# The opening of a two-layer kernel on one NeuronCore: another order for the heads' projections, and layer 1's modulation rows moved to the last leg of attention

## The reference

```
mod = (silu(c) @ wmod).reshape(2, 6, 1, 128)      # sa, ca, ga, sb, cb, gb; ga and gb clamped away from 0
h   = layernorm(x) * (1 + ca) + sa
q, k, v = h @ Wq.T, h @ Wk.T, h @ Wv.T            # 16 heads of width 8
x   = x + ga * softmax(q k^T / sqrt(8)) v
h   = layernorm(x) * (1 + cb) + sb
x   = x + gb * coupling(h)                        # three cycles of a small gelu network and a twist of h
```

## Time and profile before

| | us |
|---|---|
| median of three runs | 1130.92 |
| profiled execution, its own time | 1132.08 |
| its span | 1130.5 |
| mean granted TensorE clock, share of full speed | 0.952 |

### The profile page before, as it was taken

How to read it: one execution, slowest core, us unless ns; L and a number is a source line. 1 busy time by engine, 2 the same in 40 slices (tenths; PEclk the granted TensorE clock), 3 DMA queues, 4 the chain that set the end, 5 groups by cost and what they waited for, 6 DMA issues and landing times. The chain is left out here.

```text
span 1130.5 us, 21410 instructions
## 1 busy us (share of the span) xinstructions
PE 1032.9 (91%) x7835; PEld 647.7 (57%) x7835; DVE 969.4 (86%) x1327; ACT 817.1 (72%) x1593; POOL 518.1 (46%) x487
## 2 busy tenths in 40 slices
PE   6899999999999787989999998899999996499997
PEld 4212222222222233458988885468988984398887
DVE  6889999999995686979999996989999999876766
ACT  3279998999999544978888853988988833246642
POOL 5400441010101121027899982038999984146663
PEclk9769999999999998799999999899999997799999
DMA  5210100001004420108999990108999977612223
GB/s 158 71 40 20 28 18 17 30 16 31 16 2 76 132 57 2 59 1 194 241 246 229 221 213 1 60 22 191 232 246 238 231 185 258 130 54 65 63 63 126
DMA packets 60311, 121.03 MB, mean 107 GB/s; under 512 B 15470, under 2 KB 28782, under 8 KB 59952
## 3 DMA queue, kind: packets, MB, share of 16 engines
q0 software_dynamic: 15440, 52.66, 23.3%
q1 hardware_dynamic: 43034, 64.81, 18.5%
q10 hardware_dynamic: 1734, 2.20, 0.6%
HBM read 58.02 MB, written 13.19 MB: 63 GB/s over the span
## 5 line engine op out<-in xcount | busy, mean ns | idle before, releaser
L2268 PEld LDWEIGHTS m_pair<-filter_w,delta_x_t 128*128 128x128 f32 x2560 | 294.0, 192 | 42.1 <-issue 42.1
L2268 PE MATMUL m_pair<-filter_w,delta_x_t 128*128 128x112 f32 (+3 forms) x2560 | 298.5, 276 | 8.8 <-DVE h_t L2295 3.3
L570 DVE TENSOR_REDUCE neg_max<-max_ps 128x1 f32<-128x1024 f32 x256 | 293.1, 1212 | 10.2 <-PE max_ps L559 10.0
L687 ACT ACTIVATE exp_scores<-score_k 128x512 f32<-128x512 f32 x512 | 273.8, 600 | 19.6 <-PE score_k L679 12.4
L2244 ACT ACTIVATE decay<-delta,a_log 128x1024 f32<-128x1024 f32 x128 | 145.7, 1141 | 49.0 <-DVE normed L2295 28.9
L559 PE MATMUL max_ps<-k_rows,q_rows 48*128 48x512 bf16 x512 | 165.8, 402 | 8.3 <-DVE neg_max L570 7.6
L2236 ACT ACTIVATE filter_w<-filter,b_t 128x112 f32<-128x112 f32 (+1 forms) x576 | 167.4, 374 | 0.0
L707 PE MATMUL score_k<-exp_scores,v_cols 128*32 128x256 f32 x2048 | 164.5, 395 | 0.0
L679 PE MATMUL score_k<-q_rows,k_rows 51*128 51x512 bf16 x512 | 163.5, 390 | 0.0
L579 POOL CAST neg_max_parts<-neg_max 128x16 bf16<-128x16 f32 x16 | 3.1, 197 | 227.8 <-DVE neg_max L570 227.8
L559 PEld LDWEIGHTS max_ps<-k_rows,q_rows 48*128 48x128 bf16 x512 | 29.8, 95 | 120.6 <-DVE neg_max L570 92.6
(11 more groups left out here) (343 smaller groups left out, 1716.3 us busy)
## 6 DMA issues: line engine op xcount, KB each, us to landing
c_row<-c_rows SPq DMA_DIRECT2D x64, 512.0 KB, 6.0
x_inner<-normed POOLq DMA_DIRECT2D x16, 512.0 KB, 6.5
delta_x<-mod_memory POOLq DMA_DIRECT2D x15, 512.0 KB, 8.5
delta_x<-x_inner POOLq DMA_DIRECT2D x15, 512.0 KB, 8.3
x_inner<-h_t POOLq DMA_DIRECT2D x14, 512.0 KB, 6.4
mod_memory<-h_t POOLq DMA_DIRECT2D x14, 512.0 KB, 9.0
mod_memory<-normed POOLq DMA_DIRECT2D x12, 512.0 KB, 8.9
gate_up_all<-in_gate_up_w SPq DMA_DIRECT2D x8, 512.0 KB, 7.4
```

The costliest lines, as they stand in the source:

```text
L570: ve.tensor_reduce(nm[leg % 2][:, 4 * j + qt:4 * j + qt + 1], mps[:, bank:bank + 2, :].rearrange("p a q -> p (a q)"), AX_X, ALU.max, negat ...
L687: ac.activation(pt[a % 4][:, HEADS[r % 4], :], eps[:, bank, :], ACT.Exp, scale=SC).then_inc(*exped.up())
L2268: mm = pe.matmul(vps[blk][:, lo:hi], self.duT[b][:, c, blk * P:(blk + 1) * P], wf[g % 3][:, lo:hi], start=True, stop=True)
```

## The change

It changes the order and the place of work, not what is computed.

1. x of the first batch is loaded in two halves, then the identity and the coupling weights, then the second batch. Statistics, roots and the first eight normalised tiles follow in halves, ahead of the modulation's columns. Layer 1's modulation inputs are loaded after the identity's copy on ACT.
2. The first batch's q and k are split in another division: one middle part on DVE, three on ACT; three low parts on POOL, the last on DVE. Chunk 1 is turned by ACT. Parts of heads 0 to 3 are written out and read back first (all reads issued by SP), those of heads 4 to 15 behind them.
3. All turning, projecting and values of the second batch stand ahead of the first maximum; the 22 tiles ahead are then one stretch. The second batch's middle and low parts and its write to DRAM stand behind.
4. Layer 1's modulation rows, columns, `po_finish_rows(1)` and clamped gate columns leave the front and legs 4 and 5 and go into the last leg, places 0 to 3; the rows are copied out of PSUM by DVE.

`sp_gate_rows` stays where it is.

```diff
+        for half in range(2):
+            lo = half * TB // 2
+            sp.dma_start(self.X[:, lo:lo + TB // 2, :], A["L0_attn_x"][0][lo * P:(lo + TB // 2) * P].rearrange(
+                "(k p) d -> p k d", p=P)).then_inc(*self.in_x[half].up(16))
+        sp.dma_start(self.ident[:], A["k_ident"]).then_inc(*self.in_k.up(16))
...
-            self.ac_load_modulation(1)
...
-            self.ac_silu_c(1)
...
+            self.ac_load_modulation(1)
+            half = TB // 2
+            roots = [self.ln_root(self.X, i * half, (i + 1) * half, [self.in_x[i].at()]) for i in range(2)]
+            self.po_spread(0)
+            normed = [self.ve_ln_apply(self.X, t, roots[t // half]) for t in range(TB)]
+            self.ve_mod_cols(0, cols_ps)
+            scaled = self.m_scale
+            root = self.ln_root(self.X, TB, NT, [self.in_x[2].at()])
...
+                def first_batch_parts():
+                    tiles, rest_in = [(c, side) for c in range(2) for side in range(2)], []
+                    for n, tile in enumerate(tiles):
+                        bank = ring.take()
+                        pe_project(*tile, bank)
+                        ac_part_hi(*tile, bank)
+                        rest_in.append(ve_part_rest(*tile, bank))
+                        if n == 0:
+                            po_part_lo(*tile, ve_part_mid(*tile, rest_in[0]))
+                        if n > 1:
+                            po_part_lo(*tiles[n - 1], ac_part_mid(*tiles[n - 1], rest_in[n - 1]))
+                    ve.wait_ge(*self.ln_aggr.at())
+                    ve_second_batch_normed(range(TB, TB + TB // 2))
+                    ve_part_lo(*tiles[3], ac_part_mid(*tiles[3], rest_in[3]))
+                    ve_second_batch_normed(range(TB + TB // 2, NT))
...
-                for c in range(2):
-                    project(c)
+                first_batch_parts()
                 for c in range(2):
                     values(c)
-                sp_parts_out(0)
-                rows_in[0] = [self.mod_row(0, j) for j in range(4)]
+                sp_parts_out(0, range(4), ((part_hi.at(),), (part_mid.at(), part_ve.at()), (part_po.at(), part_ve.at())))
...
                 for part in range(3):
                     load_first(sp, kp, 1, part)
-                    load_first(ac if part < 2 else sp, qp[:].rearrange("d s a q -> d s (a q)"), 0, part)
+                    load_first(sp, first_q, 0, part)
                 sp_load(0, 1)
-                po.wait_ge(*part_lo.at())
-                po_value_columns()
-                ve.wait_ge(*self.ln_aggr.at())
-                normed += [self.ve_ln_apply(self.X, t, root) for t in range(TB, NT)]
-                self.turn(normed, col(1), col(0), (scaled,), done=ht, by=(0, 0, 0, 1), chunks=(2, 3))
-                rows_in[1] = [self.mod_row(1, j) for j in range(4)]
-                self.ve_mod_cols(1, self.pe_mod_cols(1))
-                ahead(0)
-                project(2)
-                ahead(1)
-                ahead(2)
-                project(3)
+                sp_parts_out(0, range(4, H), ((), (), ()))
+                for j in range(4):
+                    bank = ring.take()
+                    self.pe_mod_row(0, j, bank)
+                    rows_in[0].append(self.ac_mod_row(0, j, bank))
+                turned(2)
+                second_batch_parts(2, 0)
+                turned(3)
+                second_batch_parts(2, 1)
+                for side in range(2):
+                    second_batch_parts(3, side)
                 for c in range(2, NC):
                     values(c)
-                sp_parts_out(1)
-                po.wait_ge(*part_lo.at())
+                self.ac_silu_c(1)
+                for tile, rest_in in rest_known:
+                    po_part_lo(*tile, ac_part_mid(*tile, rest_in))
+                self.po_spread(1)
+                po_value_columns()
                 po_ones(2, NS)
+                for v in range(AHEAD):
+                    ahead(v)
...
+                sp_parts_out(1, range(H), ((part_hi.at(),), (part_mid.at(),), (part_po.at(),)))
...
-                if place == 3:
-                    if leg in (2, 4):
-                        self.po_finish_rows(leg // 2 - 1, rows_in[leg // 2 - 1])
...
-                    if leg in (3, 5):
-                        self.ve_mod_gates(leg // 2 - 1)
+                if place == 3 and leg == 2:
+                    self.po_finish_rows(0, rows_in[0])
+                    m_row0 = self.gate_rows.at()
+                if place == 3 and leg == 3:
+                    self.ve_mod_gates(0)
+                    m_col0 = self.m_col
+                if leg == NLEG - 1:
+                    if place == 0:
+                        ring.bind([mps[:, k, :] for k in range(4)])
+                        pe.wait_ge(*max_read.at())
+                    if place < 2:
+                        for j in (2 * place, 2 * place + 1):
+                            bank = ring.take()
+                            self.pe_mod_row(1, j, bank)
+                            rows_in[1].append(self.ve_mod_row(1, j, bank))
+                    elif place == 2:
+                        self.ve_mod_cols(1, self.pe_mod_cols(1))
+                        self.po_finish_rows(1, rows_in[1])
+                    else:
+                        self.ve_mod_gates(1)
 
             self.ht, self.attn_normed = [], normed
             self.sp_gate_rows()
-            self.ve_coupling_columns()
-            ring.bind([mps[:, k, :] for k in range(4)])
-            pe.wait_ge(*max_read.at())
+            self.ve_coupling_columns(m_row0)
             turn_in(0)
             results(NLEG - 1)
```

More of the change, by code:

```diff
@@ L763, in ahead @@
                 if v == NU + 1:
-                    for m in ring.out():
-                        pe.wait_ge(*m)
+                    pe.wait_ge(*ring.out()[0])
+                    pe.wait_ge(*self.identb_set.at())
                     max_turn(0)
+                    for part in range(3):
+                        sp.wait_ge(*to_dram[0][part].at())
+                    sp.wait_ge(*rows_set.at())
                     for half in range(2):
@@ L882, in attention @@
+                self.po_spread(1)
+                po_value_columns()
+                po_ones(2, NS)
+                for v in range(AHEAD):
+                    ahead(v)
+                for m in ring.out():
+                    pe.wait_ge(*m)
+                sp_parts_out(1, range(H), ((part_hi.at(),), (part_mid.at(),), (part_po.at(),)))
             gated = self.sig("attn_gated")
-            pe.wait_ge(*self.identb_set.at())
-            for v in range(3, AHEAD):
-                ahead(v)
```

122 lines of the change are left out of this document (61 added, 61 removed).

## The result

The changed kernel takes **1139.9 us** (median of 6, 1137.07 to 1142.38) beside 1130.57 for the kernel before (6 runs, 1126.36 to 1133.19): ratio 1.0083, 95% interval 1.0066 to 1.0100, so 9.3 us slower. Its profiled execution took 1138.03 us, span 1136.7, at a mean granted clock of 0.948. The forecast of 1136.5 had the sign right. The measured time lies only 0.1 us inside the upper end of its range (1129.5 to 1140.0) and 0.4 us above the forecast's own range. Against the medians the loss was forecast as 5.6 us and measured as 9.3.

The account below looks back on a forecast made before the run. The prediction took the attention loop's fixed pace, then a chain into coupling, as the bound. From the median 1130.92, - 4.4 (earlier loop) + 9.4 (late swaps) + 0.6 (low clock) gave 1136.5 us, range 1129.5 to 1140.0.

Parts of the forecast that it names:

- The front: Before the attention loop: exponentials begin 4.4 us earlier, 0.7 from the first reduction and 3.7 from sixteen maxima in one stretch.
- x in halves: At the kernel's start: the first chunk is turned by about 11.3 us instead of 12.46, 1.1 us earlier.
- draw: On PE ahead of the first reduction: removing layer 1's rows (4.45 us) balances adding four projections of 0.63 x 2.
- The last leg: At the attention loop's end: layer 1's rows and columns cost PE 2 us, free by themselves because something else is later.
- POOL: In the last leg: POOL finishes layer 1's rows (11.05 us) ahead of the last divide, so DVE gates 2.9 us late.
- SP's queue: At attention's end: the gate rows' write ahead of the swaps makes coupling start 9.4 us later, bounds 4.4 and 10.5.
- Behind it: At coupling's start: PE's next products may run at the low clock, adding 0.6 us, bounds 0 and 2.
- The swaps slip past: Rival, before coupling: the write's traffic doesn't hold the swaps, coupling is only 4.4 us late, 1131.5 us; chance 0.15.
- Absorbed: Rival, in coupling: shorter waits for later swaps take back up to 7.4 of the 9.4 us, 1128.5 us; chance 0.13.
- The front brings nothing: Rival, before the loop: late reads or a clock fall shrink the gain there to 1 us, 1139.9 us; chance 0.10.

## Why the prediction was right, and where it was short

**The front** was right in all its steps. First reduction 30.81 (31.2 predicted), one stretch at 1.18 us, first exponential 56.62 (56.7). Both of its terms are there: 1.1 us at the first reduction (0.7) and 3.4 from the sixteen in one stretch (3.7). With the spread of such landmarks the closeness to a tenth is luck; the 3.6 us over all seven executions lie within the bounds of 2 and 6. The x in halves was put at 1.1 us; the first turned chunk starts at 10.29 for the 11.68 of the earlier trace rows, 1.4 us. The "draw" between the rows and four projections held; the experiment with the rows in front shows what it rests on. With rows, columns and projections all ahead of the first product, the first reduction comes 4.0 us later.

**The last leg** was mis-sized: 2 us for the three blocks on PE, 1.08 + 1.67 + 1.51 = 4.3 measured. The step named a cover ("score banks are filled ahead of ACT") and did not price it. And it was put down as free by itself but for 0.6 us at the root. The term left out DVE: the copies of the rows stand in its queue ahead of the reciprocal that the root hangs on (3.3 us late, shown above).

**A term was missing, in the change's favour:** the gates of layer 1 leave leg 5, where they cost 1.7 us. The page's exponentials alone don't show it; the spacing of one leg's value products against the next would have. From the first exponential to the last value product the loop took 311.2 us against 308.0: + 4.3 for the blocks, - 1.7 for the gates, about - 1.1 for the low stretch of the clock (it reached 10.3 us into the loop instead of 12.8, and ACT is only some half as busy in it), and + 1.7 spread over legs 3 to 5 (20.9, 19.7 and 19.2 us, where 20.5, 18.8 and 18.8 would be the old pattern with one stall). The clock goes with most of that (columns as above):

```profile
138.60:142.00 3.40, 3.40 (x26) 0.56 (x24) 2.81 (x3) 2.85 (x6) 0.00 (x0) 0.50 0.00 0
```

Right behind the stall of leg 3's gates, in which PE idled 1.6 us, the granted clock is low from 138.57 to 141.98, across the end of leg 3. Seven of the experiments' kernels show such a fall behind a stall of the gates; the leg at whose end it lies takes 20.5 to 21.2 us and the next one 19.5 to 20.9. The kernel before and the one without layer 1's columns have the stall and no fall, and every leg of theirs but the stalled ones and the last takes 18.8 or 18.9. Legs 3 and 4 are 1.3 us of the 1.7; the last 0.4, in leg 5, stays open.

**POOL** was right in mechanism and in its 11 us (362.45 to 373.65), and 2.7 us late: 373.65 for 371.0. Its root ended at 362.5 where the working gives 360.0, held by the reciprocal behind DVE's copies; that is read from the trace, and no run tests it.

**SP's queue** was right in place and sign and 3.2 us short: from the write's first issue to the start 16.6 us for the 13.4 worked out. The other two measurements of it are 15.1 (the write alone) and 17.0 (late rows in the old front). The first 1.2 us are a reading: 12.7 us was the end of the traffic in the earlier trace rows, but the write's last DMA landed at 361.60, 13.9 us after the first issue. The landings of the earlier trace rows had no other transfers behind them; here the four swaps and mamba's weights follow at once, the write's landings grow to 6.2, 10.1 and 13.6 us (least, median, most), and its last is 16.1 us after the first issue, 2.2 more. All of it shares 187 GB/s on average from 373.68 to 390.00. The second half of the swap landed 0.5 us behind the write (0.7 in the sum). The sum had let the ends of the two overlap; they lengthen each other. The start at 390.32 is thus 5.9 us behind the 384.4 forecast: 2.7 + 3.2.

**Behind it** the sum had + 0.6 for the clock. In the profiled execution coupling lost 1.6 us more up to its last sum of x, and then 6.2 us came back: 2.8 in mamba's opening, 1.8 in the scan, 1.6 after it. This is why the profiled executions differ by 5.95 us while the medians differ by 9.3. The forecast of 5.6 looks exact beside the first figure, and that is partly luck: two steps were short by 5.9 us and later stages returned as much in that execution. The other profiles settle a part of it. Mamba's opening (from the last sum of x to the scan's first product) takes 62.8 to 63.0 us in all three kernels whose first swap came late, and 64.2 to 66.1 in the nine others, so some 2 us return whenever coupling starts late. The 1.8 us in the scan are absent from the kernel with late rows in the old front (431.7 us, as before). The medians' difference of 9.3 lies above the profiled executions' 5.95 by 3.4 us, as much as the stages from the scan on returned here, so the medians speak against that part as a rule.

**The rivals.** "The swaps slip past" falls: 9.8 us of wait. "Absorbed" falls: the waits for later swaps did not shrink (17.2 - 9.8 = 7.4 us, as in the earlier trace rows). "The front brings nothing" falls, though its time of 1139.9 is the one measured: its number came out by another way, which shows that a median alone tells no mechanism.

## What to carry to other kernels

A write that nobody waits for can be the dearest item of a change, if it is put where transfers that somebody does wait for follow: count its bytes and its landing, and look at what is issued in the next 15 us on any queue. Work moved out of a gap into a loop that runs at the pace of one engine costs nearly its full length there (4.3 of 4.6 us on PE, 1.7 of 2.0 on DVE), even for ten operations on two columns; and it delays what stands behind it in its engine's queue. Before moving something, look whether anything reads it.

## What the runs showed of the hardware

- Four DMAs of 512 KB that write to DRAM in rows of 512 bytes take 4.2 to 5.4 us of SP's time. With swaps issued right behind them, the user of the first swap runs 15.1 to 17.0 us after the write's first issue; all transfers together move 187 GB/s in the change (373.68 to 390.00). Written from POOL's queue, they make the user of SP's swaps wait 14.8 us.
- DMAs of one queue don't land strictly in the order of issue: in all three kernels with the swaps behind the write, the first swap half landed 1.5 to 2.3 us before the write's last DMA (388.22 and 389.77 in the change).
- The issue itself is slower behind such a backlog: four swap halves took 2.46 us of SP on a free queue and 5.53, 6.02 and 6.08 us behind the write.
- Operations of DVE on 128x2 (with a scalar or between two tensors) came every 0.20 us, so ten of them are worth 1.6 reductions of a 128x1024 tile.
- The clock can fall to its lower level while PE is busy throughout: 362.5 to 369.0 us in the kernel with the gate rows last, behind twelve products of two columns, and again in the kernel with the gate rows on POOL's queue; the same products in the change were followed by no fall.
